# A causal attention stage with a staggered score loop: the third key blocks of two heads share a PSUM bank, the eviction of results and the projections change places

## The reference

```python
h = xn @ W1 + b1                              # q, k, v of 16 heads, d = 8
w = einsum('bhqd,bhkd->bhqk', q, k) / sqrt(d)
w = softmax(w * mask - (1 - mask) * 1e6)      # mask = tril
a = einsum('bhqk,bhkd->bhqd', w, v)
out = x + (a @ Wp + bp) + ffn(xn)             # ffn: routed top 2 of 8, and shared
```

## Time and profile before

| | us |
|---|---|
| median of 3 runs | 562.68 |
| lowest, highest | 562.01, 566.24 |
| profiled execution, its own time | 566.17 |
| its span, first to last instruction | 564.4 |
| mean granted PE clock in it | 0.919 |

### The profile page before, as it was taken

One profiled execution on the slowest core, in us unless ns is written; L12 is line 12 of the kernel. 1 busy time (PEld: TensorE's weight loads), 2 busy tenths in 40 slices (PEclk: granted clock), 3 DMA queues, 4 the chain that ended last, 5 costly groups with the idle time before them and its releaser, 6 DMA issues.

```text
span 564.4 us, 13835 instructions
## 1 busy us (share of the span) xinstructions
PE 514.6 (91%) x4547; PEld 339.3 (60%) x4548; DVE 394.3 (70%) x753; ACT 310.3 (55%) x684; POOL 323.1 (57%) x382
## 2 busy tenths in 40 slices
PE   6578999989999899898998898999999999999995
PEld 3334445445454444543544247999999999977673
DVE  6776678897978778787778455555555555548896
ACT  2016777777777777777767543333333333355542
POOL 5567542342558758677678622676675544475442
PEclk9755999999989899898979659999999999999997
DMA  7614431130111524613101101221122122334554
GB/s 210 187 39 160 170 143 63 41 133 21 59 58 66 215 66 171 184 54 133 49 30 39 50 23 58 62 67 59 56 70 61 56 63 68 112 109 120 157 155 149
DMA packets 51867, 53.45 MB, mean 95 GB/s; under 512 B 5456, under 2 KB 39280, under 8 KB 51568
## 3 DMA queue, kind: packets, MB, share of 16 engines
q1 hardware_dynamic: 46752, 42.97, 23.9%
q0 software_dynamic: 4352, 8.95, 4.8%
q10 hardware_dynamic: 720, 0.93, 0.5%
HBM read 20.38 MB, written 17.90 MB: 68 GB/s over the span
## 4 chain that ended last, share of the span: by engine, by line
PE 69%; DVE 11%; ACT 8%; issue 6%; DMA 3%; ACTq 1%; DVEq 1%; POOL 1%; SPq 0%; POOLq 0%
PE av_bank L855 15%; PE av_bank L1017 9%; PE mx_pair L800 9%; PE st_banks L828 5%; DVE neg_max L1507 5%; ACT probs L1204 4%; PE st_banks L1028 4%; DVE o_sb L1682 3%; PE mx_pair L1003 2%; DMA out<-o_sb 2%; PE st_banks L738 2%; PE mx_pair L1005 2%; PE mx_pair L1007 2%; PE mx_pair L1008 2%; PE mx_pair L1006 2%
## 5 line engine op out<-in xcount | busy, mean ns | idle before, releaser
L1507 DVE TENSOR_REDUCE neg_max<-mx_pair 128x2 f32<-128x256 f32 (+3 forms) x256 | 203.0, 822 | 63.2 <-PE mx_pair L811 61.7
L1204 ACT ACTIVATE probs<-st_banks 128x512 f32<-128x512 f32 (+1 forms) x384 | 181.3, 526 | 75.8 <-PE st_banks L828 75.2
L828 PE MATMUL st_banks<-q_st,k_st 32*128 32x128 f32 (+3 forms) x512 | 98.9, 416 | 17.8 <-ACT probs L1204 16.8
L684 POOL DMA_INDIRECT y_tok<-y_sb,y_rows x72 | 70.0, 972 | 76.6 <-ACT y_sb L1313 61.8
L800 PEld LDWEIGHTS mx_pair<-k_st,q_st 31*128 31x128 f32 x512 | 45.3, 196 | 99.8 <-DVE neg_max L1507 55.8
L800 PE MATMUL mx_pair<-k_st,q_st 31*128 31x256 f32 (+3 forms) x512 | 91.9, 404 | 13.9 <-DVE neg_max L1507 9.8
L855 PE MATMUL av_bank<-probs,v_wide 128*18 128x512 f32 (+3 forms) x1024 | 100.3, 491 | 0.0
L828 PEld LDWEIGHTS st_banks<-q_st,k_st 32*128 32x128 f32 x512 | 49.8, 195 | 36.8 <-ACT probs L1204 23.6
L610 POOL DMA_INDIRECT sorted_x<-xn_rows,slot_idx x64 | 63.2, 987 | 13.3 <-issue 12.7
L569 POOL TENSOR_SCALAR_AFFINE_SELECT probs<-probs 128x1024 f32<-128x1024 f32 x32 | 34.8, 1087 | 57.1 <-ACT probs L1204 57.1
L1306 ACT ACTIVATE sg<-mx_pair 128x352 f32<-128x352 f32 x72 | 33.4, 463 | 61.7 <-PE mx_pair L1008 61.7
(11 more groups left out here) (214 smaller groups left out, 885.6 us busy)
## 6 DMA issues: line engine op xcount, KB each, us to landing
sorted_x<-zeros SPq DMA_DIRECT2D x8, 580.5 KB, 4.4
xg<-sorted_x SPq DMA_DIRECT2D x36, 129.0 KB, 2.2
q_st<-q_hi SPq DMA_DIRECT2D x16, 256.0 KB, 2.4
picked<-y_tok SPq DMA_DIRECT2D x16, 256.0 KB, 3.7
k_st<-k_hi SPq DMA_DIRECT2D x14, 256.0 KB, 2.8
egu_lo<-in_e_gu SPq DMA_DIRECT2D x2, 1408.0 KB, 7.4
x_all<-in_x SPq DMA_DIRECT2D x8, 256.0 KB, 4.8
q_st<-q_lo SPq DMA_DIRECT2D x8, 256.0 KB, 2.7
```

The costliest lines, as they stand in the source:

```text
L684: pool.indirect_dma_start(y_tok, bass.IndirectOffsetOnAxis(ap=y_rows[:, t, k:k + 1], axis=0), y_sb[t % 2][:, k, :], None).then_inc(y_st[t ...
L828: ins = pe.matmul(st_banks[:, i % 3, lo:lo + w], k_st[buf][32 * j:32 * j + 32, g, kb * P:(kb + 1) * P], q_st[buf][32 * j:32 * j + 32, g, k ...
L1204: act.activation(dst, src, ACT.Exp, scale=SCALE).then_inc(st_free, 1)
L1507: ins = dve.tensor_reduce(neg_max[:, g, h:h + 2, qb], mx_pair[i % 2][:, :, lo:lo + (qb + 1) * P], AX.X, ALU.max, negate=True)
```

## The change

Six edits. (1) Units 8 to 11 become two, THIRD = 8 and THIRD + 1 = 9, each a whole bank with two heads: unit 8 holds heads 0 and 1, unit 9 heads 2 and 3, 256 columns each. (2) They are filled over two visits: at visit 5 `third_scores(s, 0)` writes heads 2 and 0 into the first halves of the two banks, at visit 6 `third_scores(s, 1)` writes heads 3 and 1 into the second halves, after PE's own semaphore `third_half` says that the first two matmuls are complete. Only then are the banks full. (3) ACT evicts them with two Exp of 512 columns instead of four of 256, both behind visit 6. (4) `values(s-1, 2)` moves from in front of visit 4 to behind it. (5) All fills of `second_misc` move from behind visit 5 to behind visit 4, so that visits 5 and 6 follow each other. (6) `results_out_of` moves to the end of the step on ACT, behind the last exponents. `mask_third` waits for the Exp of unit 8 (the last one).

```diff
-ST_PARTS = [[(0, 0)], [(3, 0), (1, P)], [(2, 0)]]
+ST_PARTS = [[(0, 0)], [(3, 0), (1, P)]]
+THIRD = 8
...
-        scored = [("S", s, u) for u in (2, 3, 0, 1, 6, 7, 4, 5, 10, 11, 8, 9)] if s >= 0 else []
-        order += scored[0:4] + ([("m", s + 1)] if -1 <= s < GROUPS - 1 else []) + scored[4:8] + first_misc(s) + scored[8:10] + second_misc(s) + scored[10:12]
+        scored = [("S", s, u) for u in (2, 3, 0, 1, 6, 7, 4, 5, THIRD + 1, THIRD)] if s >= 0 else []
+        order += scored[0:4] + ([("m", s + 1)] if -1 <= s < GROUPS - 1 else []) + scored[4:8] + first_misc(s) + second_misc(s) + scored[8:10]
...
+            def third_scores(n, k):
+                b, g = divmod(n, NG)
+                buf = b % NBUF
+                w = S - 2 * P
+                if k == 1:
+                    pe.wait_ge(third_half, 2 * (n + 1))
+                for half in (1, 0):
+                    i, j = ST_NO["S", n, THIRD + half], 2 * half + k
+                    if k == 0:
+                        pe.wait_ge(st_free, i - 2)
+                    pe.matmul(st_banks[:, i % 3, k * w:(k + 1) * w], k_st[buf][32 * j:32 * j + 32, g, 2 * P:3 * P],
+                              q_st[buf][32 * j:32 * j + 32, g, 2 * P:S], start=True, stop=True,
+                              skip_group_check=True).then_inc((third_half, st_full)[k], 1)
...
                 if valued:
                     values(s - 1, 3)
-                    values(s - 1, 2)
                 if maxima:
                     max_scores(s + 2, 3)
                 if scored:
                     scores(s, (4, 5))
                 if maxima:
                     max_masks(s + 2, 3)
+                if valued:
+                    values(s - 1, 2)
...
-                if maxima:
-                    max_scores(s + 2, 4)
-                if scored:
-                    scores(s, (10, 11))
-                if maxima:
-                    max_masks(s + 2, 4)
...
                 if maxima:
+                    max_scores(s + 2, 4)
+                if scored:
+                    third_scores(s, 0)
+                if maxima:
+                    max_masks(s + 2, 4)
+                if maxima:
                     max_scores(s + 2, 5)
                 if scored:
-                    scores(s, (8, 9))
+                    third_scores(s, 1)
                 if maxima:
                     max_masks(s + 2, 5)
...
-                if s >= 1 and s % GP == 0:
-                    results_out_of(s - 1)
                 if scored:
                     exponents(s, (4, 5))
...
-                if scored:
-                    exponents(s, (10, 11))
...
                 if scored:
-                    exponents(s, (8, 9))
+                    exponents(s, (THIRD + 1, THIRD))
+                if s >= 1 and s % GP == 0:
+                    results_out_of(s - 1)
```

More of the change, by code:

```diff
@@ L56 @@
 NMX = 6
-ST_PARTS = [[(0, 0)], [(3, 0), (1, P)], [(2, 0)]]
-NST = 12
+ST_PARTS = [[(0, 0)], [(3, 0), (1, P)]]
+THIRD = 8
 PRIME_HID, PRIME_HIDT, PRIME_Y = 1, 2, 3
@@ L305, in attention_moe_kernel @@
         st_full, st_free, mx_full, mx_free = (sem(n) for n in ("st_full", "st_free", "mx_full", "mx_free"))
+        third_half = sem("third_half")
         mask_set, mask_ld = sem("mask_set"), sem("mask_ld")
@@ L573, in mask_third @@
                 diag = probs[n % 2][:, 8:10, :].rearrange("p u (h w) -> p (u h) w", h=2)[:, :, 0:P]
-                pool.wait_ge(st_free, used_up("S", n, 9))
+                pool.wait_ge(st_free, used_up("S", n, THIRD))
                 pool.affine_select(out=diag, in_=diag, compare_op=ALU.is_ge, fill=0.0, base=0,
@@ L1195, in exponents @@
                     act.wait_ge(st_full, i + 1)
-                    src, w = st_banks[:, i % 3, :], 2 * P
+                    src = st_banks[:, i % 3, :]
                     if u < 4:
                         dst = probs[n % 2][:, u, :]
-                    elif u < 8:
+                    elif u < THIRD:
                         dst, src = probs_by_block[n % 2][:, :, u - 4, :], src.rearrange("p (c w) -> p c w", w=P)
                     else:
-                        dst = probs[n % 2][:, 8 + (u - 8) // 2, u % 2 * w:(u % 2 + 1) * w]
-                        src = src[:, 0:w]
+                        dst = probs[n % 2][:, u, :]
                     act.activation(dst, src, ACT.Exp, scale=SCALE).then_inc(st_free, 1)
```

## The result

| | before | after |
|---|---|---|
| median | 562.95 us (4 runs, 562.01 to 566.24) | 582.98 us (4 runs, 577.70 to 586.89) |
| ratio, 95% interval | | 1.0312 (1.0262 to 1.0361) |
| profiled execution, span | 566.17, 564.4 | 584.22, 582.5 |
| mean granted clock | 0.919 | 0.920 |

The change makes the kernel 3.1% slower. The forecast was 576 us (564 to 586) with slower at 0.71: sign and range hold, the size is 7 us short. In the profiled executions, against which the sum was made, it is +18.1 us where +13.6 stood.

The account below looks back on a forecast made before the run. PE was taken to set the pace from first values to projection, the PE-DVE-ACT hand-over from visit 5 to the next first values. Step losses of 13.1 us plus 0.5 for early steps, on the 562.7 median, gave 576 us (564 to 586).

Parts of the forecast that it names:

- The gate: Score pair (4,5) starts 0.14 us behind unit 6's Exp; block 2's values, free before it, cost 0.52 us behind.
- The results at the end: In even steps the next step's first values wait for ACT's eviction of results, about 0.3 us a step.
- The wait on `third_half` and the masks: From visit 5: PE's wait for PE costs 0.1 us (0 to 0.14); masks end 0.77 behind the first maxima.
- The sum: Attention steps by kind add 4.8, 2.7, 3.6 and 2.0 us, together 13.1; with 0.5 for the first four, +13.6.
- the 0.5 for fills: First four steps, where misc fills also leave their cover: 0.5 us added (0 to 3).
- rivals 1 and 3: Clock drops in the attention: the first has all go, 567 us, chance 0.12; the other seven to ten more, 586, 0.11.
- 2, ACT's stalls as the bound: In the handover two evictions for four remove Exp waits, first values 0.4 us earlier: 551 us, chance 0.09.
- 4, the 0.52 taken back later: The two visits cost nothing, 0.52 us returns later in the step; results' wait alone stays, 4 us: 567, chance 0.08.

Follow-up runs that it names:

- the move: Kernel before with key block 2's values moved behind visit 4 and the eviction of results behind the Exp (4,5): ratio 1.0078.
- its undoing: Changed kernel with key block 2's values back in front of visit 4, results still at the step's end: 584.77 us, ratio 1.0190.
- the second chip: Kernel before and changed kernel, neither edited, run again on another chip: 573.03 and 592.80 us, 1.0345 by the medians.
- the mixed kernel: Kernel before with third blocks sharing banks only in the 18 steps without a second fill, nothing moved: 556.21 us, ratio 0.9886.

## Why the prediction was right, and where it was off

**The gate.** Confirmed three times: by after (265.16), by the kernel without block 2's product, whose steps don't get shorter, and by the move (+0.44 to +0.57 in three kinds of step, forecast 0.52; the results stand behind the Exp of (4,5) there as well) and its undoing (-0.36 to -0.56). That steps without a projection lose nothing by it did not hold: they lose 0.2 and more in the move's kernel.

**The results at the end.** Alone they cost +0.22 and +0.17 in even steps, where about 0.3 was expected. PE waits 4.5 us in all for them; the same group of before has an idle time of 0.0. This is the page's group of the values in the changed kernel (busy us, mean ns, idle before):

```profile
L871 PE MATMUL av_bank<-probs,v_wide 128*18 128x512 f32 (+3 forms) x1024 | 105.9, 489 | 4.7 <-ACT av_sb L1233 4.5
```

**The wait on `third_half` and the masks.** In step 22 visit 5's maxima start at 267.26 and the second halves at 267.92. The first half in unit 8 ends at 267.54 + 0.33 = 267.87, so the second halves follow it by 0.05 us, and the wait of PE for PE costs little there (0 to 0.14 bounded, 0.1 taken). How much of the 0.05 is the wait is not shown, as PE has visit 6's maxima in front of the second halves. I took 0.8 for the step with the halves at 0.85 behind visit 5, and 0.66 as the value if they come 0.2 earlier; they come 0.66 behind it and the step loses 0.67. The Trainium skill (TensorEngine Tiling (Array Packing), Restrictions and Gotchas) forbids two row tiles in one bank at the same time. All kernels here that share a bank keep to it by that wait, so no run shows what a breach does; the rows show that keeping to it is cheap (0.05 us).

**The sum.** Over steps 6 to 29, seven steps without, and five each with values (9 to 25), queries and keys, the measured differences of the table, each taken for all steps of its kind, give 7 x 0.30 + 5 x (0.68 + 0.67 + 0.45) = 11.1 us; by the forecast's values it is 7 x 0.25 + 5 x (0.6 + 0.8 + 0.45) = 11.0. In steps 2 to 5 it is 3.3 (0.68 + 0.40 + 1.57 + 0.68), against 2.1 and the 0.5 for fills. Step 4, with a router piece in front of visit 5, is the one that stands out; the fills' move alone gave it 0.81.

**The term that was mis-sized** is the clock, for which the sum had none (it stood in rivals 1 and 3 alone), and with it the start, taken as 0.5 beside the steps. Of the +8.2 us before step 6, 1.1 come before step 1 (0.8 of it stand already at visit 1 of step -2, 22.39 against 21.59, before anything of the change runs) and 3.7 in step 1, which runs at half clock until 65.7 us where before is at full clock from 56.7 on. Of the +15.8 between steps 6 and 30, 4.7 are not in the table: 41.0 us at half clock there against 24.7 before, that is 4.8 drops of 3.4 us more, at 1.34 us 6.4, more than enough to hold it. From step 30 on the changed kernel has 0.98 where before had 0.94, and gets 6.0 us back. Steps 10 and 11 together (+1.00) lie near the table (+1.12). So the terms of the mechanism make 14.4 us (3.3 + 11.1), near the 13.6 forecast, and the clock and the start the rest, as the balance of +1.1, +3.7, +4.7 and -6.0 (+3.5, to the rounding of these figures). That this balance is small, and the time inside the range, is luck: without the 6.0 us given back in the tail it would be 589. The two profiles of the second chip have another balance, +5.4 us before step 6, +8.0 from there to step 30 and -0.4 behind it, as the kernel before has the stall there.

**The rivals.** *1 and 3, fewer or more drops:* in the stretch from 60 to 340 us the two kernels have 47.8 and 46.7 us at half clock. Neither all went nor did seven to ten come on top, but rival 3 is right for the steps: 4.8 drops more between steps 6 and 30, which the tail gives back. On the second chip the same stretch has 51.2 and 61.4 us. The price of a drop, 1.2 us in both rivals, is 1.34 to 1.46. *2, ACT's stalls as the bound:* false for the change, where no kind of step gets shorter, but its germ is true. Sharing a bank gives 0.10 to 0.15 us in a step whose visits 5 and 6 have nothing between them; it was priced at nothing in the forecast, with the ACT time saved. The advice of the Trainium skill (TensorEngine Tiling (Array Packing), PSUM Bottleneck) to vectorize PSUM access over tiles in one bank therefore holds in sign in the plain steps (7.66 against 7.79 us), and the mixed kernel collects it; in steps with a fill between the visits it costs (9.73 against 8.89). *4, the 0.52 taken back later:* refuted at full clock by every kind of step with a projection, though on chips with the stall a part of it is indeed taken back.

Not tried: the changed kernel without drops of the clock, as no edit here removed them all; so that the clock explains the 4.7 us is worked out from the price of one drop and not shown. Why the drops come where they do is open.

## What to carry to other kernels

Before work is moved off the path in front of a gate, find out what releases the gate: an instruction that starts a fixed time (here 0.14 us) behind the end of another engine's instruction is gated, and work in front of it is free up to the length of the wait, while the same work behind it costs its full length where the engine walks on. Take the good part of a bundle alone and put it only where its neighbours allow: shared banks with values and results moved lose 3.1%, shared banks in the 18 plain steps win 1.1%. A sum of undisturbed steps was reliable to some tenths of a microsecond per kind of step (forecast and table differ by 0.13 at most), but the clock adds or takes back several us on top, so a total within 1% can't be read from it.

## What the runs showed of the hardware that was not expected

- Less work can be slower: with 256 fewer matmuls the kernel took 1.0104 times as long, with unchanged steps and a mean clock of 0.900 to 0.920 in place of 0.920 to 0.935.
- A clock drop at half speed for 3.4 us costs a step 1.34 to 1.46 us. With filler in the idle stretches in front, four of them were gone, and two others appeared later.
- The same kernel takes 562.5 us on one chip and 573 to 575 on three others. From step 14 on the others show 0.9 to 1.3 us in most even steps, in place of 0.2, between the end of the values on PE and the eviction that they release. Why is open.
- A second matmul into a bank that another row group has just written to started 0.05 us behind the first one's end, with a semaphore between them (step 22 of after).
